# Wait numbers in 16-bit rows, and a gate product as scalar-tensor-tensor, in a three-layer graph network

## What is computed

```
h   = relu(layernorm(x))
h   = normalized rows of gcn_conv(h, W1)                    # sum over edges, 1/sqrt(degree) on both ends
ev  = sigmoid(h[src] @ We1[:H] + h[dst] @ We1[H:] + be1)     # one gate for each edge
na  = relu(segment_sum(ev * h[src], dst) @ Wn1 + bn1)
ev2 = sigmoid(na[src] @ We2[:H] + na[dst] @ We2[H:] + be2)
g   = relu(segment_sum(ev2 * na[src], dst) @ Wn1 + bn1)
out = x + gcn_conv(g, W2, weights ev2)
```

## Time and profile before

| | before |
|---|---|
| time, median of three | 3128.99 us |
| profiled execution, first to last instruction | 3140.2 us |
| PE matmul busy | 2590.4 us (82%) |
| DVE busy | 2084.8 us (66%) |
| POOL busy | 1876.4 us (60%) |
| ACT busy | 1647.7 us (52%) |
| mean granted TensorE clock | 0.939 |

### The profile page before, as it was taken

One profiled execution on the slowest core, in us unless ns is written; L12 is line 12 of the kernel. 1 busy time (PEld: TensorE's weight loads), 2 busy tenths in 40 slices (PEclk: granted clock), 3 DMA queues, 4 the chain that ended last, 5 costly groups with the idle time before them and its releaser, 6 DMA issues.

```text
span 3140.2 us, 59452 instructions
## 1 busy us (share of the span) xinstructions
PE 2590.4 (82%) x16470; PEld 2270.1 (72%) x16470; DVE 2084.8 (66%) x6198; ACT 1647.7 (52%) x3374; POOL 1876.4 (60%) x1812
## 2 busy tenths in 40 slices
PE   0777779888897878787899999999999877687776
PEld 0444448888885767677788888888888677676775
DVE  4687886566526666666775666766666567676766
ACT  7576666666666555555554444444444533333333
POOL 5366576556305777777702766666662177777773
PEclk9899999999998898998999999999999988989888
DMA  4255555555532333343313444444442333333333
GB/s 120 84 188 184 185 190 204 203 202 203 186 144 84 118 111 108 122 123 107 119 62 103 147 133 130 137 134 127 139 137 85 131 125 103 122 108 120 108 120 90
DMA packets 185600, 419.63 MB, mean 134 GB/s; under 512 B 36656, under 2 KB 136701, under 8 KB 175534
## 3 DMA queue, kind: packets, MB, share of 16 engines
q10 hardware_dynamic: 83703, 244.23, 21.9%
q0 software_dynamic: 61472, 140.49, 15.5%
q1 hardware_dynamic: 40118, 31.23, 3.2%
HBM read 311.35 MB, written 102.16 MB: 132 GB/s over the span
## 4 chain that ended last, share of the span: by engine, by line
PE 49%; POOL 15%; DMA 12%; issue 10%; DVE 5%; ACT 5%; ACTq 2%; DVEq 0%; SPq 0%; POOLq 0%
POOL rows L615 14%; PE ps L1150 12%; DMA rows<-table,edge_src 11%; PE ps_high L1142 8%; PE ps_high L1150 8%; PE ps L1082 7%; ACT tab_area L782 3%; PE ps_high L1099 3%; PE ps L1062 2%; PE ps_high L1094 2%; PE ps_high L1229 1%; DVE tab_area L1553 1%; ACTq L394 1%; PE ps L1262 1%; POOL acc L599 1%
## 5 line engine op out<-in xcount | busy, mean ns | idle before, releaser
L615 POOL DMA_INDIRECT rows<-table,edge_src x1664 | 1780.9, 1070 | 941.7 <-SPq L513 435.1
L1142 PE MATMUL ps_high<-rows,weights 128*128 x2784 | 620.6, 338 | 296.1 <-SPq L510 129.3
L1150 PE MATMUL ps<-tab_area,acc 128*128 128x129 f32 (+2 forms) x4410 | 820.5, 326 | 0.2
L1625 DVE TENSOR_TENSOR acc<-acc 128x640 f32<-128x640 f32 x735 | 604.1, 822 | 210.4 <-ACT acc L891 197.0
L1142 PEld LDWEIGHTS ps_high<-rows,weights 128*128 128x128 f32 x2784 | 468.1, 204 | 375.5 <-DVE weights L1595 160.9
L1150 PEld LDWEIGHTS ps<-tab_area,acc 128*128 128x128 f32 x4410 | 696.3, 206 | 44.0 <-DVE acc L1608 2.9
L882 ACT ACTIVATE step<-xbuf,rows 128x128 f32 x928 | 358.2, 394 | 622.1 <-PE ps_high L1142 400.6
L1150 PE MATMUL ps_high<-tab_area,acc 128*128 128x129 f32 (+2 forms) x2940 | 585.2, 325 | 0.0
L782 ACT ACTIVATE tab_area<-ps_high x816 | 403.3, 494 | 208.7 <-PE ps_high L1099 169.0
L1150 PEld LDWEIGHTS ps_high<-tab_area,acc 128*128 128x128 f32 x2940 | 477.4, 206 | 28.2 <-DVE acc L1608 1.3
L1608 DVE TENSOR_TENSOR acc<-acc,ps_high 128x129 f32 (+1 forms) x948 | 333.7, 352 | 211.4 <-PE ps_high L1142 199.7
(11 more groups left out here) (241 smaller groups left out, 2180.2 us busy)
## 6 DMA issues: line engine op xcount, KB each, us to landing
acc<-counts ACTq DMA_DIRECT2D x105, 1120.0 KB
counts<-tab_area ACTq DMA_DIRECT2D x51, 1568.0 KB, 6.3
acc<-counts ACTq DMA_DIRECT2D x25, 1568.0 KB
rows<-table,edge_src POOLq DMA_INDIRECT x1664
table<-tab_area SPq DMA_DIRECT2D x6, 903.0 KB, 4.7
table<-acc SPq DMA_DIRECT2D x7, 448.0 KB, 4.2
table<-tab_area SPq DMA_DIRECT2D x6, 455.0 KB, 3.8
table<-tab_area SPq DMA_DIRECT2D x6, 448.0 KB, 3.0
```

Of the source, the lines that this page charges most:

```text
L615: nc.gpsimd.indirect_dma_start(rows[:, t % UNROLL, 0:row_floats[k]], None, tables[k], bass.IndirectOffsetOnAxis(ap=edge_src[:, t:t + 1], a ...
L1142: nc.tensor.matmul(ps[DENSE_BANKS + m % PAIR_BANKS][:, 0:WIDTH[k]], weights[:, m % W_RING, :], rows[:, bass.ds(known["slots"][m % UNROLL], ...
L1150: ins = nc.tensor.matmul(ps[j][:, 0:WIDTH[k]], gate_blocks[:, n % S_RING, j * PART:(j + 1) * PART], table[:, h, 0:WIDTH[k]], start=(h == 0 ...
L1625: nc.vector.tensor_tensor(block, block, count_in[n // CHUNK % 2][:, :, n % CHUNK, :], ALU.mult)._wait_ge(gated, n + 1).then_inc(blocks_rea ...
```

## The change

Two edits. The product of gates and counts is issued as a scalar-tensor-tensor, (gates * 1.0) * counts, with the same operands and waits. And the numbers that are only waited on lie in 16-bit rows: `entry_row` becomes u16, and a copy of part 2 of `pair_row`, `pair_need` (u16), is made by one more DVE copy in the setup; every load of part 2 reads it.

```diff
-        entry_row = sb("entry_row", [1, LAG - 1 + HALF], i32)
+        entry_row = sb("entry_row", [1, LAG - 1 + HALF], u16)
+        pair_need = sb("pair_need", [1, HALF_PAIRS], u16)
...
+        def pair_part(part, at):
+            return pair_need[0:1, at] if part == 2 else pair_row[0:1, part, at]
...
         def load_pairs(engine, k, part, i, top):
-                pair_row[0:1, part, i * UNROLL:(i + 1) * UNROLL], engines=[engine], min_val=0, max_val=top,
+                pair_part(part, slice(i * UNROLL, (i + 1) * UNROLL)), engines=[engine], min_val=0, max_val=top,
...
         def load_eight(engine, part, i, top, step=1):
-                pair_row[0:1, part, i * 2 * QUAD + step - 1:(i + 1) * 2 * QUAD:step], engines=[engine], min_val=0, max_val=top,
+                pair_part(part, slice(i * 2 * QUAD + step - 1, (i + 1) * 2 * QUAD, step)), engines=[engine], min_val=0, max_val=top,
...
             chain(both(pair_row[:, 2, :], ps[6][0:1, 0:HALF_PAIRS], -1.0, 1.0, ALU.mult, ALU.add))
+            nc.vector.tensor_copy(pair_need[:, :], pair_row[:, 2, :])
...
-                    nc.vector.tensor_tensor(block, block, count_in[n // CHUNK % 2][:, :, n % CHUNK, :],
-                                            ALU.mult)._wait_ge(gated, n + 1).then_inc(blocks_ready, 1)
+                    nc.vector.scalar_tensor_tensor(block, block, 1.0, count_in[n // CHUNK % 2][:, :, n % CHUNK, :],
+                                                   ALU.mult, ALU.mult)._wait_ge(gated, n + 1).then_inc(blocks_ready, 1)
```

## The result

The changed kernel takes 3158.39 us (median of 4 runs, 3154.64 to 3164.66) where the kernel before takes 3128.61 (4 runs, 3124.41 to 3137.01): ratio 1.0084, 95% interval 1.0061 to 1.0107. It is 0.8% slower, 30 us; the forecast was 23 us faster, and 3158 lies above its range. Its profiled execution spans 3156.2 us at a mean clock of 0.93.

What follows compares the result with a forecast made beforehand. It took PE to bound pass 2, POOL's gathers passes 1 and 3, and PE's idle time behind slow needs to lengthen pass 0. Terms -23 - 1 + 1 = -23 us took 3129 to 3106 us, range 3085 to 3145.

Steps and rivals of the forecast that it cites:

- If a trip is 16 bytes, the load takes one trip ... I take -23 us.: Pass 0, PE's load of two needs: 16-bit numbers need one trip, not two; -23 us, bounds 0 and -30.
- the kind answer: Pass 0: the case that the two needs come in one trip, 3090 to 3119 us; chance 0.48.
- ACT ... to about 600, PE ... to about 650, SP ... to about 580: Loads of 16 numbers shorten at 16 bits, from 1022, 1105 and 972 ns; 78 us together, only -1 us uncovered.
- the second rival: Register loads: narrow numbers are fetched one by one, a load of 16 needing 16 trips; 3150 to 3230 us, chance 0.13.
- Almost all is covered ... in pass 2 by PE's full queue.: Shorter loads outside pass 0's needs are hidden, by POOL in passes 1 and 3, PE's queue in 2; -1 us left.
- Pass 3 ... +20 to +60: The second rival in pass 3: 4.9 us of PE loads every 16 pairs fill PE and drop its clock; +20 to +60 us.
- SP's loads ... +0 to +10: The second rival in pass 0: SP's loads reach 10 us; +0 to +10 us.
- The product: +1, the same hold.: DVE's scalar-tensor-tensor costs the same as tensor-tensor and holds POOL's gathers alike; +1 us, from 0 to +19.
- The copy in the setup: nothing.: Setup: the added DVE copy of 464 numbers, under 1.09 us, precedes a 4.67 us wait and costs nothing.
- The mechanism of pass 0: Pass 0: slow needs idle PE 2.13 us and the clock often halves, making such stretches 2.8 us longer.

Runs made afterwards that it cites:

- b4: The changed kernel with ACT's 16 slots from a 16-bit row too, one standstill 7.8 us in place of 5.4: 3307.0 us, ratio 1.0560.
- a3: The changed kernel with ACT's loads of 16 needs in passes 1 and 2 from the 32-bit row again: 3138.4 us, ratio 1.0012.
- a4: The changed kernel with PE's loads of 16 needs in pass 3 from the 32-bit row again: 3150.4 us, ratio 1.0062.
- a2: The changed kernel with SP's entries (`entry_row`) in 32 bits again: 3160.3 us, ratio 1.0089.
- e2: e1 with SP's entries alone in 16-bit rows: 3102.3 us, ratio 0.9894 to the kernel before.
- a1: The changed kernel with the product as a tensor-tensor again, the 16-bit rows kept: 3159.8 us, ratio 1.0086.
- e1: b1 with PE's pass 0 needs loaded for four quads at once, four 32-bit neighbours: 3101.7 us against 3132.7, ratio 0.9889.
- b1: The changed kernel with every waited-on number from 32-bit rows again, the scalar-tensor-tensor product kept: 3133.8 us, ratio 1.0007.
- b2: b1 with pass 0's needs in a 32-bit row of their own, so a load's two numbers are neighbours: 3136.3 us, ratio 1.0014.
- b3: The changed kernel with ACT's 16-bit needs loaded four at a time in place of sixteen: 3131.9 us, ratio 1.0002.

## Why the prediction was wrong

- **"If a trip is 16 bytes, the load takes one trip ... I take -23 us."** This step failed: the trip was taken to be counted in bytes. Two 16-bit numbers take two trips (528 ns, up to 2.5 us in the burst); the term is 0, and the stretches stayed where they were. The rows had left this open, as the text said, and 0.48 went to the kind answer.
- **"ACT ... to about 600, PE ... to about 650, SP ... to about 580".** The same step in other places: 3385, 3793 and 3255 ns. This is the second rival, which had 0.13. Its prices held: +2.4 us on ACT (measured 2.36), +2.7 on PE (2.69), +2.3 on SP (2.28), and so did its range, 3150 to 3230. The page Runtime: NRT & Kernel Launch of the Trainium skill, section "Instruction fetch mechanics", gives some 200 ns a register even in bulk, for the register loads that the runtime adds. For 16-bit, shifted and strided numbers the traces now agree (203 to 237 ns); for aligned groups of four they don't (16 in 1.0 to 1.1 us).
- **"Almost all is covered ... in pass 2 by PE's full queue."** Wrong in its reason. A full TensorE isn't cover; it is the place where a lost moment can't be made up, and pass 2 has 15 of the 30 us. Nor was POOL the cover that the text took it for in passes 1 and 3: pass 3 lost 6 to 9 us to PE's loads, and b4's pass 1 lost 56 to ACT's. In pass 2 the cover is the blocks made ahead. The rival put its end at two steps, 5.6 us; a3, the changed kernel and b4 show that a piece of 3.1 us is free, 5.4 costs 0.5 us and 7.8 costs 3.6.
- **"Pass 3 ... +20 to +60"** (the rival). Right in direction and too large: 6 to 9 us by a4 and the traces, in a pass where TensorE has 24% of idle time.
- **"SP's loads ... +0 to +10"** (the rival). 0 on the chips of a2 and e2, where the kernel before takes the time of the forecast; 32 us on two others.
- **The product: +1, the same hold.** Right: 821 against 822 ns, a gather still ends 0.82 us behind it, and a1 is unchanged. The Vector Engine (DVE) Microarchitecture Reference of the Trainium skill, section "Points that are easy to get wrong", would have halved its rate; the trace doesn't agree.
- **The copy in the setup: nothing.** Right; it takes 390 ns.
- **The mechanism of pass 0** (slow needs idle PE for 2 us, and the clock falls to 0.92) was read rightly: e1 made it happen and gained 31 us, where the bound given was 30. Some 6 of them it owes to the half of its loads that are gone, which was no part of the forecast.

What stays open is a part of pass 1. On the chips of a, b and e it takes 609 to 613 us where ACT stands still for 5.4 us (the changed kernel, a1, a2, a4), 665 where it stands for 7.8 (b4), and 596 to 608 where no standstill is over 3.1 us (before, a3, b1, b2, b3, e1, e2). So the standstill costs this pass too; why the kernels of the last kind differ by 12 us among themselves, no experiment took apart.

## What to carry to other kernels

Price a register load by its trips, not by its bytes: keep such numbers at 32 bits, in groups of four whose start is aligned (a start 4 bytes off made all of them come one by one), and where few are wanted pack them so that four come together. Judge a load in an engine's queue by the length of one standstill against the work made ahead of it, not by the sum of its loads, and look first at the passes in which the engine that waits is full. Where the trace has no row for an operand's width, both prices stay open, and the dear one deserves as much of the chance as the kind one.

## What the runs showed of the hardware

- A register load costs 0.2 to 0.26 us a trip. A trip brings an aligned group of four 32-bit numbers (0.31 to 0.34 us for one group, 0.97 to 1.1 for four) or one number of another kind: sixteen at 16 bits 3.25 to 3.8 us, sixteen at 32 bits and 4 bytes off 3.27, eight with a step of two 1.73, two neighbours 0.546.
- In the burst of count tiles loads are slowed, those of two trips by twice as much as those of one: in e1 334 ns became 1.3 to 1.4 us, in the changed kernel 528 ns up to 2.5 and SP's 3.25 up to 7.1 us.
- The same kernel took 3131, 3133, 3276 and 3306 us on four chips. The change cost 0.8% in its first measurement and 2.8% on the chip of the 3276. The kernel with four needs a load won on all three chips on which it ran (3133, 3276, 3306), by 0.7 to 1.1%.
